# Scan layers: B reaches the diagonals of its blocks by DMA through a cleared DRAM buffer

## The reference, cut to what matters

```python
proj = seq @ W_proj.T + b_proj              # 192 x, 192 delta, 16 B, 16 C
delta = softplus(delta + dt_bias)
# for every token t, channel d and state n:
h = exp(d_t[..., None] * A) * h + (d_t * x_t)[..., None] * b_t[:, None, :]
y_t = einsum('bdn,bn->bd', h, c_t)
y = y + x_in * D
out = y @ W_out.T + b_out
```

## Time and profile before

| what | value |
|---|---|
| median of 3 runs | 4304.23 us (4302.74 to 4306.74) |
| the profiled execution, its span | 4308.6 us |
| TensorE matmul | 3710.7 us busy, 86% |
| VectorE | 3432.3 us, 80% |
| GpSimd | 2659.4 us, 62% |
| ScalarE | 2105.8 us, 49% |
| DMA, main queue | 295440 packets, 408.35 MB, 41.7% of 16 engines |

### The profile page before, as it was taken

One profiled execution on the slowest core, in us unless ns is written; L12 is line 12 of the kernel. 1 busy time (PEld: TensorE's weight loads), 2 busy tenths in 40 slices (PEclk: granted clock), 3 DMA queues, 4 the chain that ended last, 5 costly groups with the idle time before them and its releaser, 6 DMA issues.

```text
span 4308.6 us, 119610 instructions
## 1 busy us (share of the span) xinstructions
PE 3710.7 (86%) x49136; PEld 2266.0 (53%) x49136; DVE 3432.3 (80%) x3492; ACT 2105.8 (49%) x2803; POOL 2659.4 (62%) x973
## 2 busy tenths in 40 slices
PE   4994899899999996789889888899898888888897
PEld 4994666666666664344444444444444444444443
DVE  6564567667576663699998998999999989999997
ACT  2331343444444443556555555555565555555563
POOL 1111121111211210599899999999999999999998
PEclk9997899999999998799999999999999999999999
DMA  9624142242332330553543543544535535435433
GB/s 101 85 44 108 54 124 81 85 119 70 95 109 69 105 91 25 120 116 79 125 106 83 125 102 92 125 94 103 122 84 120 112 79 124 109 79 130 103 87 83
DMA packets 296948, 416.40 MB, mean 97 GB/s; under 512 B 31369, under 2 KB 185741, under 8 KB 296385
## 3 DMA queue, kind: packets, MB, share of 16 engines
q1 hardware_dynamic: 295440, 408.35, 41.7%
q10 hardware_dynamic: 978, 0.34, 0.0%
HBM read 267.09 MB, written 91.16 MB: 83 GB/s over the span
## 4 chain that ended last, share of the span: by engine, by line
PE 27%; DVE 16%; issue 12%; ACT 3%; POOL 1%; DVEq 1%; DMA 0%; ACTq 0%; POOLq 0%
DVE ssm_h L1136 11%; PE ssm_u_ps L818 10%; PE ssm_y_ps L831 10%; PE ssm_scratch L848 4%; DVE ssm_b_diag L1160 3%; PE ssm_scratch L858 1%; DVE ssm_stats L1143 1%; POOL ssm_h L1216 1%; ACT ssm_decay L967 1%; PE ssm_u_ps L893 1%; DVE ssm_y_sb L1165 1%; ACT ssm_xn L994 1%; PE ssm_scratch L873 1%; PE ssm_scratch L867 0%; DVEq L1128 0%
## 5 line engine op out<-in xcount | busy, mean ns | idle before, releaser
L1216 POOL TENSOR_TENSOR ssm_h<-ssm_h,ssm_c_rep 128x2048 f32<-128x2048 f32 x384 | 1745.4, 4550 | 107.3 <-DVE ssm_h L1136 99.6
L967 ACT ACTIVATE ssm_decay<-ssm_delta_rep,ssm_a_neg 128x1024 f32<-128x1024 f32 x768 | 863.7, 1145 | 592.1 <-DVE ssm_h L1136 589.3
L818 PE MATMUL ssm_u_ps<-ssm_b_diag,ssm_dx_t 64*64 64x128 f32 x24576 | 865.7, 282 | 262.3 <-DVE ssm_h L1136 182.6
L818 PEld LDWEIGHTS ssm_u_ps<-ssm_b_diag,ssm_dx_t 64*64 64x64 f32 x24576 | 696.3, 137 | 698.9 <-issue 694.6
L1136 DVE TENSOR_TENSOR_SCAN ssm_h<-ssm_decay,ssm_h,ssm_u_ps 128x512 f32<-128x512 f32 x768 | 944.3, 1257 | 132.5 <-PE ssm_u_ps L818 131.4
L1136 DVE TENSOR_TENSOR_SCAN ssm_h<-ssm_decay,ssm_u_ps 128x512 f32<-128x512 f32 x768 | 887.2, 1195 | 35.8 <-ACT ssm_decay L967 16.9
L831 PE MATMUL ssm_y_ps<-ssm_h,ssm_state_sum 128*64 128x512 f32 x3072 | 798.1, 643 | 8.0 <-POOL ssm_h L1216 8.0
L1752 ACT ACTIVATE l_probs<-l_work 128x532 f32<-128x532 f32 (+1 forms) x384 | 217.6, 567 | 560.7 <-PE l_work L1606 554.0
L1160 DVE TENSOR_TENSOR ssm_b_diag<-ssm_b_t,ssm_lane 128x2048 f32<-128x2048 f32 x128 | 454.0, 3549 | 22.7 <-ACT ssm_b_t L1022 22.7
L2004 POOL TENSOR_TENSOR l_rstd<-l_var_eps,l_minus_half 96x2 f32<-96x2 f32 x16 | 11.1, 695 | 586.6 <-DVE l_var_eps L1841 586.6
L831 PEld LDWEIGHTS ssm_y_ps<-ssm_h,ssm_state_sum 128*64 128x64 f32 x3072 | 196.8, 144 | 326.3 <-issue 311.9
(11 more groups left out here) (163 smaller groups left out, 5554.7 us busy)
## 6 DMA issues: line engine op xcount, KB each, us to landing
ssm_c_rep<-ssm_c_by_state SPq DMA_DIRECT2D x256, 512.0 KB, 6.5
ssm_delta_rep<-ssm_delta SPq DMA_DIRECT2D x384, 128.0 KB, 5.9
l_qk_parts<-l_qk SPq DMA_DIRECT2D x48, 768.0 KB, 4.8
ssm_x<-x_after_l SPq DMA_DIRECT2D x32, 768.0 KB, 5.8
ssm_x_res<-x_after_l SPq DMA_DIRECT2D x192, 128.0 KB, 4.3
l_x<-x SPq DMA_DIRECT2D x64, 192.0 KB, 9.1
x_after_l<-l_x SPq DMA_DIRECT2D x64, 192.0 KB, 4.1
l_x<-x_after_l SPq DMA_DIRECT2D x16, 768.0 KB, 5.5
```

The source lines that it names most:

```text
L818: made = nc.tensor.matmul(u_ps[64 * par:64 * par + 64, ring("u", w), r, at:at + 128], dx_t[rows, db, 2 * win + k, 64 * g:64 * g + 64], b_d ...
L967: nc.scalar.activation(decay[:, 2 * (s % 2) + npi, :], delta_rep[:, db, :], ACT.Exp, scale=a_neg[:, n.layer, col:col + 1]).then_inc(decay_ ...
L1216: nc.gpsimd.tensor_tensor(view, view, c_rep[:, 2 * q:2 * q + 2, :], ALU.mult).then_inc(c_applied, 1)
```

## The change: what it does

A DRAM buffer `b_diagonals` [4, 2, 64 x 2050] is filled with zeros once, by a DMA from a constant, in the first step of the attention. It can be seen in two ways: with a row pitch of 2048 values, as 64 rows of a square arrangement, and with a pitch of 2050, where the same column of every row lies two values further on, on the diagonal. For each image SP stores B from `b_t` into the second view, eight DMAs (4 npq x 2 halves of the partitions) of 64 rows x 16 pieces x 2 values. The zeros between stay. When all eight have landed, SP loads the first view into `b_diag`, two DMAs of 64 rows x 2048 values for each npq. The four VectorE products, the mask `lane` and its load are dropped; `fill_u` waits for `diag_loaded[npq]` in place of `diag_made`.

In `late` the eight stores stand behind `load_delta(m, 0)`, and the load of block 0 behind `load_delta(m, 1)`, which itself now comes ahead of `load_c(m, 0)`; the other three blocks stand between and behind the C loads.

```diff
+DIAG_ROW = 16 * 128
-def ssm_layers(nc, x_src, x_dst, w2, w3, consts, images):
+def ssm_layers(nc, x_src, x_dst, w2, w3, consts, images, diag_dram):
...
+        by_diagonal = diag_dram.rearrange("n r (j k) -> n r j k", k=DIAG_ROW + 2)
+        by_row = diag_dram[:, :, 0:64 * DIAG_ROW].rearrange("n r (j k) -> n r j k", k=DIAG_ROW)
...
+                def store_diagonals(n):
+                    await_drained(sp, fill(n, "bt"))
+                    for npq in range(4):
+                        for r in range(2):
+                            b = b_t[64 * r:64 * r + 64, :].rearrange("p (c m) -> p c m", c=16)[:, :, 2 * npq:2 * npq + 2]
+                            sp.dma_start(by_diagonal[npq, r, :, 0:DIAG_ROW].rearrange("j (c x) -> j c x", c=16)[:, :, 0:2],
+                                         b).then_inc(diag_stored, 16)
+
+                def load_diagonals(n, npq):
+                    if npq == 0:
+                        sp.wait_ge(diag_stored, n.count(128, 128))
+                        sp.sem_inc(diag_store_seen, 1)
+                    if not n.first:
+                        sp.wait_ge(u_filled, n.count(8 * S_STEPS, 8 * (npq - 3)))
+                    for r in range(2):
+                        sp.dma_start(b_diag[64 * r:64 * r + 64, npq].rearrange("p c a m -> p (c a m)"),
+                                     by_row[npq, r]).then_inc(diag_loaded[npq], 16)
...
                     store_c(n)
+                    store_diagonals(n)
                     sp.wait_ge(c_stored, 32)
                     load_c(n, 0)
+                    for npq in range(4):
+                        load_diagonals(n, npq)
                     load_c(n, 1)
...
                         store_c(m)
                         load_delta(m, 0)
+                        store_diagonals(m)
+                        sp.wait_ge(decay_made, n.count(TILES_S, 16))
+                        sp.sem_inc(rep_free, 1)
+                        load_delta(m, 1)
+                        load_diagonals(m, 0)
                         sp.wait_ge(c_stored, m.count(32, 32))
                         sp.sem_inc(c_store_seen, 1)
                         load_c(m, 0)
-                        sp.wait_ge(decay_made, n.count(TILES_S, 16))
-                        sp.sem_inc(rep_free, 1)
-                        load_delta(m, 1)
+                        load_diagonals(m, 1)
                         load_c(m, 1)
+                        load_diagonals(m, 2)
+                        load_diagonals(m, 3)
...
                     if db == 0 and win == 0:
-                        pe.wait_ge(diag_made, n.count(4, npq + 1))
+                        pe.wait_ge(diag_loaded[npq], n.count(32, 32))
...
-                def diagonals(n, npq):
-
-                    if npq == 0:
-                        await_drained(dve, fill(n, "bt"))
-                    b = b_t[:, :].rearrange("p (c m) -> p c m", c=16)[:, :, 2 * npq:2 * npq + 2]
-                    b = b[:, :, None, :].to_broadcast([128, 16, 64, 2])
-                    m = lane[:, :].rearrange("p (j i) -> p j i", i=2)[:, None, :, :].to_broadcast([128, 16, 64, 2])
-                    nc.vector.tensor_tensor(b_diag[:, npq].rearrange("p c a (j i) -> p (c a) j i", i=2), b, m,
-                                            ALU.mult).then_inc(diag_made, 1)
...
                     scan(n, w // 2, w % 2, 0)
-                    if w in (17, 19, 21, 23) and not last:
-                        diagonals(after(n), w // 2 - 8)
                     scan(n, w // 2, w % 2, 1)
...
+                    if n.first:
+                        sp.dma_start(diag_dram.rearrange("n r k -> (n r) k"),
+                                     consts["zeros"].to_broadcast([8, 64 * (DIAG_ROW + 2)])).then_inc(diag_cleared, 16)
+
+                def tail(n_next):
+                    store(n_next)
+                    sp.wait_ge(diag_cleared, 16)
```

More of the change, by code:

```diff
@@ L536, in ssm_layers @@
         ident = sb("ident", [128, 128])
-        lane = sb("lane", [128, 128])
         state_sum = sb("state_sum", [128, 64])
@@ L580, in ssm_layers @@
         dx_made = sem("dx_made")
-        diag_made = sem("diag_made")
+        diag_stored = sem("diag_stored")
+        diag_store_seen = sem("diag_store_seen")
+        diag_loaded = [sem(f"diag_loaded{npq}") for npq in range(4)]
         rows_seen = sem("rows_seen")
@@ L690, in res_rows @@
             return t.rearrange("(q c) h w -> c q (h w)", c=64)[:, :, HALF * e:HALF * e + HALF]
-        N_FIRST, N_REST = 14, 11
+        N_FIRST, N_REST = 13, 11
         def of_slot(n, name):
@@ L1109, in _ @@
                 act.dma_start(ident[:], consts["ident"]).then_inc(first_loaded, 16)
-                act.dma_start(lane[:], consts["lane"]).then_inc(first_loaded, 16)
                 act.dma_start(w_x[0][0:C], ws[0]["w_x"][0:C]).then_inc(first_loaded, 16)
@@ L1175, in prologue @@
                     nc.vector.tensor_scalar(a_neg[:, :, :], a_neg[:, :, :], -1.0, None, ALU.mult).then_inc(consts_made, 1)
-                    for npq in range(4):
-                        diagonals(n, npq)
                 def window(n, w):
@@ L1313, in tile_at, with attention @@
     return slice(first, first + 128)
-def attention(nc, tag, x_src, x_dst, w, consts, batches):
+def attention(nc, tag, x_src, x_dst, w, consts, batches, diag_dram):
     L, HALF = 1024, 512
@@ L1379, in attention @@
         x_loaded, res_loaded, out_stored = sem("x_loaded"), sem("res_loaded"), sem("out_stored")
+        diag_cleared = sem("diag_cleared")
         filled = sem("filled")
@@ L1560, in main @@
                         move_rows(n)
-                schedule(sp, prologue, main, store)
+                    if n.first:
[4 more added lines that the diff above has]
+                    sp.wait_ge(diag_cleared, 16)
+                schedule(sp, prologue, main, tail)
             @block.tensor
@@ L2025, in shape_constants @@
     out["state_sum"] = (p[:, None] % 64 == np.arange(64)[None, :]).astype(np.float32)
-    out["lane"] = np.repeat(p[:, None] % 64 == np.arange(64)[None, :], 2, 1).astype(np.float32)
+    out["zeros"] = np.zeros((1, 64 * (DIAG_ROW + 2)), np.float32)
     out["ones"] = np.ones((1, 2, 2, 512), np.float32)
@@ L2122, in program @@
     conv_layer(nc, "l0", x, between[0], weights["l0"], consts)
-    attention(nc, "l1", between[0], between[1], weights["l1"], consts, x.shape[0])
-    ssm_layers(nc, between[1], out, weights["l2"], weights["l3"], consts, x.shape[0])
+    diag_dram = nc.dram_tensor("b_diagonals", [4, 2, 64 * (DIAG_ROW + 2)], F32).ap()
+    attention(nc, "l1", between[0], between[1], weights["l1"], consts, x.shape[0], diag_dram)
+    ssm_layers(nc, between[1], out, weights["l2"], weights["l3"], consts, x.shape[0], diag_dram)
 def kernel(**inputs):
```

## The result

| | before | changed |
|---|---|---|
| median of the runs (lowest to highest) | 4303.48 us (4300.51 to 4306.74, 4 runs) | 4817.65 us (4809.24 to 4825.18, 4 runs) |
| ratio, 95% interval | | 1.1189 [1.1172, 1.1206] |
| span profiled | 4308.6 us | 4817.5 us |
| first, second, last pass mark | 1730.10, 1772.47, 4156.70 us | 1744.46, 1802.68, 4641.47 us |
| one of the 30 passes between | 79.5 us | 94.6 us |

The change costs 514 us. The span is the time of the profiled run, and the marks are VectorE's group statistics, once in each pass. They split the 509 us between the two spans: 14.4 before the first mark (attention), 15.8 between first and second (first pass), 30 x 15.1 = 454 in the loop, 24.1 behind the last mark, where one more turn of the pass lies beside the last pass. The question is thus what makes 15.1 us a pass.

The account below looks back on a forecast made before the run. VectorE, GpSimd and TensorE were taken as three full engines, waits changing hands; afterwards SP's DMA queue. 30 loops 22.4 us longer (672), first pass 35, last 6, clearing 5: +718, 5027 us, 5022 against the median; range 4420 to 5400.

Parts of the forecast that it names:

- R: Moment in each pass when SP begins the output's stores, GpSimd having added the third residual block; the loop is counted from it.
- the forecast's own case: Whole kernel: a supply between 2.45 and 3.6 ns a piece gives 4900 to 5195 us; chance 0.47.
- What goes: Each pass: four products leave, 14.2 us off VectorE and 8.2 off GpSimd; with nothing in their place about 71 us.
- X: Time the eight diagonal stores take in SP's queue each pass: 24.0 us, between 5.0 and 38.1.
- rival (a): Diagonal stores cost little beyond issue, 0.6 to 1.5 us each: 4427 us, or 4654 at 1.5 ns a piece; chance 0.25.
- lower bound 5.0: Diagonal stores in SP's queue: issue alone, 0.62 us a DMA, makes 5.0 us a pass.
- a supply of some 350 to 400 pieces a microsecond, whatever their size: DMA of small pieces: fixed pace, taken as 2.9 ns a piece, giving 24.0 us for the eight diagonal stores.
- The rate of the blocks: Block loads behind the stores: 226 GB/s, 4.64 us for 1 MB, 37.1 us for eight diagonal and C blocks.
- C's block 3 is there at R + 56.1 + X: Last of eight blocks in SP's queue gates GpSimd's four C products and residual sums, 21.8 us more: loop 101.9 us.
- First pass: First scan pass: stores, landing and two blocks replace the products, some 27 us later, and 8 more at the first turn.
- behind the last mark: Last pass, whose C blocks come late: 6 us.
- the clearing: Zero fill of 4.2 MB in the attention, mostly hidden: 5 us, between 0 and 37.

Follow-up runs that it names:

- e3: Changed kernel without the diagonal stores and block loads in every pass but the first: 4076.57 us, 0.9467 of the kernel before, 71.1 us a pass.
- e8: Changed kernel plus a probe at its end, 16 stores from SBUF to DRAM of 1024 pieces of 8, 64, 256 or 512 bytes: 4886.92 us.
- e5: Kernel before the change plus only the clearing DMA: 4330.14 us, ratio 1.0038.
- e7: Changed kernel with blocks 0 and 1 made by VectorE products again, blocks 2 and 3 by DMA: 4391.33 us, 1.0201 of the kernel before.
- e11: Changed kernel with blocks 0 to 2 made by VectorE products, only block 3 by DMA, its stores early: 4276.89 us, 0.9934 of the kernel before.
- e10: Changed kernel with the eight diagonal stores issued right after the x load, ahead of the residual loads: 4848.75 us, 1.1256 of the kernel before.
- e12: Changed kernel with each block stored and loaded by one DMA of 128 partitions instead of two of 64: 6965.52 us, 1.6177 of the kernel before.

## Why the prediction was right, and where not

The direction, the mechanism's kind (DMA on the path from R to the next pass) and the range held: 4818 for 5022. The range of 4420 to 5400 was wide, and the forecast's own case, 4900 to 5195, was missed. Two of its steps failed in opposite directions, and that the total is as near as 4% is luck.

**What goes: right.** 14.5 and 7.3 us off VectorE and GpSimd for 14.2 and 8.2; softplus sums at 1.27 us. The 8.2 was counted as four times the delay of a softplus sum, though there are only three in a pass; about half of what GpSimd gained came from its dx products. With nothing in their place 71.1 us a pass (e3).

**X, the stores: wrong.** 24.0 taken, 7.06 us of issue measured, 0.88 a DMA; the landing behind it is covered but for 2 us of SP's wait a pass (61.1 us in 30). This is nearest to rival (a), lower bound 5.0, and the forecast's own sign for (a), stores at 0.6 to 1.5 us each, is what came. The step that failed is "a supply of some 350 to 400 pieces a microsecond, whatever their size"; e8 shows the pace to grow with the size, 0.68 ns at 8 bytes and 2.7 at 512. The Trainium skill (DMA: Bandwidth & Descriptors, Why small descriptors are slow), against which I held rows 6 to 9, was nearer: it put X at the lower bound. The backlog of the earlier trace rows was the row that should have warned me: a supply that is fixed can't go at twice its pace.

**The rate of the blocks: right**, 222 GB/s for 226, 4.7 us a block.

**What gates, and what follows it: wrong.** "C's block 3 is there at R + 56.1 + X. GpSimd's step 3 needs it", and 21.8 us to R. Measured in the pass shown: block 2 lands at R + 53.9, and from there it is 37.0 us to the next R (3311.0 to 3347.98). I took all diagonal blocks to be early enough behind block 0, and did not look up in TensorE's program in which window each block's first u stands: two windows before its use and ahead of state sums and dx transposes on which GpSimd and VectorE depend. From the first diagonal load to the next R the forecast had 37.1 + 0.5 + 21.8 = 59.4 us; the pass shown has 64.4, the mean 94.6 - 27.3 = 67.3. From R to the first load it had 42.5 and measured are 27.3. So -15.2 and +7.9: the loop is 94.6 for 101.9, and the same working with the measured X would have given 77.9 + 7.1 = 85.0 a pass, about 30 x 9.6, some 290 us too few. The first error is partly covered by the second.

**A term left out.** TensorE's granted clock went from 0.97 to 0.89 in a pass that now has idle stretches, and its 69.6 us became 72.6. The forecast had the idle stretches, and no price for the clock behind them. Right after the idle 11.75 us above, the 32 matmuls of a u fill take 1.98 us (granted clock 0.52 from 3290.8 to 3296, nearly all at 1.2 GHz); from 3311 on, at 1.00 or 2.4 GHz, they take 1.10. In the pass shown all of the low clock lies ahead of block 2's landing, for which TensorE has to wait in any case. In others it lies behind. Here is the stretch from block 2's fill to the next R, in the pass shown and in the one whose R is 3624.31 (the columns of the earlier trace rows):

```profile
3311.08:3347.98 36.90, 35.89 (x582) 19.63 (x582) 30.57 (x28) 23.03 (x33) 33.07 (x14) 1.00 0.40 86
3678.31:3723.15 44.84, 40.24 (x582) 21.65 (x582) 30.30 (x27) 23.22 (x33) 33.27 (x14) 0.89 0.34 73
```

Block 2 is there at R + 54 in both, and the same 582 matmuls then take 8 us more. Over 29 passes, from R to R: the nine with a granted clock of 1.00 from R + 54 on last 90.5 to 93.6 us, 92.2 on average, and the seven with 0.92 or less 97.9 to 103.2.

**The rest.** First pass +15.8 for 27 and 8, since X was a third of its size; behind the last mark +24.1, of which one turn is 15, for 6; the clearing 14.4 here and 22 alone (e5), for 5. Packets 583,559 for 600,000. The marks 94.6 apart instead of 102; the waits of TensorE for DMA at each turn as told; those of GpSimd for DMA before steps 2 and 3 not there.

**Open.** How the 7.9 us behind the first load split between the order in TensorE's queue and the lower clock wasn't tried. An estimate from those 29 passes: 94.6 - 92.2 = 2.4 us for the clock and 5.5 for the order. It takes the passes at full clock for what they all would last, and that isn't shown. A version with u's fills behind the state sums would tell; that this order matters is read from the waits and from e7 and e11, and no run changes it. Why single stores take 1.7 to 4.0 us to issue, three of eight in e10 and one of eight in the pass shown, is not shown either.

## What to carry to other kernels

Before work moves from an engine to the DMA, list every consumer of what is copied in the order in which its engine's program meets it, not in the order in which the data is used: an in-order queue that works ahead needs its data earlier, and holds everything behind it. One block of four was worth moving, by 0.66%, and two or four were not, so move as much as stays behind other work, no more. Moving an entry within a queue that issues without a pause does not bring its end forward.

## What the runs showed of the hardware that I had not expected

- Small pieces from SBUF to DRAM go at 0.68 ns (8 bytes), 0.76 (64), 1.7 (256) and 2.7 (512) a piece (e8); 8192 pieces of 8 bytes, 512 bytes apart in DRAM, are issued in 7.1 us and landed 11.9 us after the first issue began.
- One DMA of 128 rows whose source has an outermost dimension of two ran at 53 GB/s for 222, the share of two engines. The kernel with its loads and stores merged so is 1.6 times as long (e12).
- Two costs on one chain weighed less apart than together: the stores 133 us without the loads, 267 with them.
- A clearing of 4.2 MB by one DMA put the first mark 17 us later (e5): in the changed kernel a copy of 768 KB issued just behind it landed after 22.3 us instead of 4.7.
- With the same 582 matmuls behind block 2's landing, a pass took 36.9 us at a granted clock of 1.00 and 44.8 at 0.89.
